# Max pass on 51 contraction rows, two heads at once on the two row halves of TensorE, in a one-core attention layer

## The reference, cut to what matters

```python
xn  = layer_norm(x, norm_w, norm_b)
q   = (xn @ q_w + q_b).reshape(8, 512, 16, 16)
k   = (xn @ k_w + k_b).reshape(8, 512, 16, 16)
att = jnp.einsum('bnhl,bmhl->bnmh', q, k) + (1.0 - mask) * -1000000.0
att = jax.nn.softmax(att, axis=2)
v   = ((xn @ v_w + v_b) * src_mask[:, :, None]).reshape(8, 512, 16, 16)
y   = jnp.einsum('bnmh,bmhl->bnhl', att, v).reshape(8, 512, 256)
h   = layer_norm(y, sb_norm_w, sb_norm_b) * (1.0 + scale) + shift     # scale, shift from silu(cond) @ emb_w
out = x + silu(h) @ out_w + out_b
```

## Time and profile before

| | |
|---|---|
| median of 3 runs | 567.2 us (567.03 to 567.59) |
| profiled execution, its own time | 564.98 us |
| its span | 563.1 us |
| TensorE busy | 96% |
| VectorE busy | 77% |
| ScalarE busy | 66% |
| GpSimd busy | 34% |
| granted TensorE clock | 1.00 throughout |

### The profile page before, as it was taken

One profiled execution on the slowest core, in us unless ns is written; L12 is line 12 of the kernel. 1 busy time (PEld: TensorE's weight loads), 2 busy tenths in 40 slices (PEclk: granted clock), 3 DMA queues, 4 the chain that ended last, 5 costly groups with the idle time before them and its releaser, 6 DMA issues.

```text
span 563.1 us, 10292 instructions
## 1 busy us (share of the span) xinstructions
PE 542.6 (96%) x2845; PEld 226.2 (40%) x2845; DVE 431.7 (77%) x906; ACT 371.2 (66%) x674; POOL 192.7 (34%) x238
## 2 busy tenths in 40 slices
PE   7798999999999999999999999999999999998986
PEld 3452343334443444434443444434443344423334
DVE  7399767987879877897869878897869878788422
ACT  2306866678656886677756786687756786676741
POOL 6433211445225421346205522336215432314003
PEclk9999999999999999999999999999999999999999
DMA  5650342424124333342225243242334223241021
GB/s 140 201 162 11 87 114 86 124 85 123 57 64 139 87 115 103 95 132 79 73 86 141 85 113 104 71 137 79 80 97 132 84 85 90 67 143 34 1 76 37
DMA packets 43433, 53.74 MB, mean 95 GB/s; under 512 B 11000, under 2 KB 36728, under 8 KB 43408
## 3 DMA queue, kind: packets, MB, share of 16 engines
q1 hardware_dynamic: 41360, 53.17, 32.9%
q10 hardware_dynamic: 2048, 0.27, 0.3%
HBM read 36.35 MB, written 16.80 MB: 94 GB/s over the span
## 4 chain that ended last, share of the span: by engine, by line
PE 64%; issue 12%; DMA 7%; DVE 5%; SPq 4%; POOL 3%; ACT 2%; ACTq 1%; POOLq 0%; DVEq 0%
PE pv_ps L414 16%; PE mx_ps L381 15%; PE st_ps L398 14%; PE job_ps L436 6%; DMA q_rows<-qk_dram 5%; PE job_ps L470 4%; PE job_ps L443 3%; SPq L977 2%; DVE negmax L659 2%; POOL qk_parts L855 2%; SPq L980 1%; PE job_ps L458 1%; ACT probs L515 1%; PE job_ps L449 1%; PE job_ps L453 1%
## 5 line engine op out<-in xcount | busy, mean ns | idle before, releaser
L659 DVE TENSOR_REDUCE negmax<-mx_ps 128x1 f32<-128x512 f32 x512 | 328.3, 679 | 74.5 <-PE mx_ps L381 71.3
L515 ACT ACTIVATE probs<-st_ps 128x512 f32<-128x512 f32 x512 | 278.3, 598 | 97.2 <-PE st_ps L398 96.5
L381 PE MATMUL mx_ps<-k_rows,q_rows 99*128 99x512 bf16 x512 | 195.6, 382 | 6.3 <-DMA q_rows<-qk_dram 5.6
L398 PE MATMUL st_ps<-q_rows,k_rows 101*128 101x512 bf16 x512 | 193.7, 381 | 3.3 <-DMA q_rows<-max_parts 1.2
L414 PE MATMUL pv_ps<-probs,v_rows 128*32 128x512 f32 x1024 | 136.4, 605 | 0.5 <-ACT probs L515 0.5
L381 PEld LDWEIGHTS mx_ps<-k_rows,q_rows 99*128 99x128 bf16 x512 | 50.3, 98 | 126.7 <-DVE negmax L659 85.8
L846 POOL TENSOR_TENSOR qk_rest<-qk_full,qk_parts 128x512 f32<-128x512 f32 x32 | 37.0, 1157 | 162.7 <-ACT qk_parts L525 162.6
L398 PEld LDWEIGHTS st_ps<-q_rows,k_rows 101*128 101x128 bf16 x512 | 49.8, 98 | 63.0 <-ACT probs L515 23.5
L855 POOL TENSOR_TENSOR qk_parts<-qk_rest,qk_parts 128x512 bf16<-128x512 f32 x32 | 37.1, 1158 | 68.7 <-DVE qk_parts L736 68.7
L436 PE MATMUL job_ps<-x_norm_t,w_qk 128*128 128x512 f32 x128 | 60.2, 591 | 0.0
L536 ACT ACTIVATE qk_full<-job_ps,qkb_col 128x512 f32<-128x512 f32 x32 | 22.0, 687 | 36.2 <-PE job_ps L436 36.2
(11 more groups left out here) (75 smaller groups left out, 387.8 us busy)
## 6 DMA issues: line engine op xcount, KB each, us to landing
qk_dram<-qk_parts SPq DMA_DIRECT2D x96, 128.0 KB
k_rows<-qk_dram SPq DMA_DIRECT2D x32, 192.0 KB
q_rows<-qk_dram SPq DMA_DIRECT2D x32, 192.0 KB
x_in<-in_x SPq DMA_DIRECT2D x16, 256.0 KB, 3.4
k_rows<-qk_dram SPq DMA_DIRECT2D x32, 128.0 KB
q_rows<-qk_dram SPq DMA_DIRECT2D x32, 128.0 KB
x_res<-in_x SPq DMA_DIRECT2D x8, 512.0 KB, 4.6
out<-out_sb SPq DMA_DIRECT2D x16, 256.0 KB, 2.2
```

What stands on the lines that cost most here:

```text
L381: pe.matmul(mx_ps[bank_of(u, MX_BANKS)][:, :], q_rows[0:ROWS_MASK, g, h, c * P:(c + 1) * P], k_rows[0:ROWS_MASK, g, h, :], start=True, sto ...
L398: pe.matmul(st_ps[bank_of(u, ST_BANKS)][:, :], k_rows[0:ROWS_ALL, g, h, c * P:(c + 1) * P], q_rows[0:ROWS_ALL, g, h, :], start=True, stop= ...
L515: act.activation(probs[:, t % P_SLOTS, h, :], st_ps[bank_of(u, ST_BANKS)][:, :], ACT.Exp).then_inc(exp_done, 1)
L659: dve.tensor_reduce(negmax[:, g % 2, h * CH + c:h * CH + c + 1], mx_ps[bank_of(GH * step + h, MX_BANKS)][:, :], AXIS_X, ALU.max, negate=Tr ...
```

## The change

The max pass now uses three of the six products (part 0 by part 0, part 0 by part 1, part 1 by part 0) and the mask: 48 + 3 = 51 rows, which fit one half (64 rows) of the array. Heads 0 and 1 of a group have their main rows from partition 0, heads 2 and 3 from partition 64. `max_pair` issues the max matmuls of two heads, one on each half, one behind the other (`tile_position=(base, 0)`), into two banks; it waits until both banks are free. The score pass still contracts all six products: for heads 0 and 1 over partitions 0 to 100, for heads 2 and 3 over 0 to 116, of which 0 to 15 are zeros. The heads go in the order 0, 2, 1, 3. A step on TensorE is now: pair, score, score, `pv_step`, MID jobs, pair, score, score, END jobs.

Since the two halves of the heads have different layouts, each fill DMA is now one per half, with 2 KB a row: 12 fills and 2 mask DMAs a group where 6 and 1 were (768 KB in all as before, 32 to 96 KB each), and 4 DMAs on ScalarE for the maxima where 2 were. The large presets of ones are gone; two small tiles are set on VectorE, and ScalarE issues six DMAs that copy them, ahead of its first activation.

```diff
+HALF = 64
+MAIN = 3 * HD
+MASK_AT = MAIN
+MAX_AT = MASK_AT + PARTS
+MAIN_ALL = MAX_AT + 2
+MAIN_BASE = (0, HALF)
+REST_BASE = (MAIN_ALL, HALF - MAIN)
+ROWS_ALL = (MAIN_ALL + MAIN, HALF + MAIN_ALL)
+ORDER = (0, 2, 1, 3)
-ROW_DMAS = 7
+ROW_DMAS = 14
+MAX_DMAS = 4
+PRESET_DMAS = 6
...
-            def max_unit(b, t, h):
+            def max_pair(b, t, j):
...
-                u = GH * step + h
-                wait(pe, max_done, UNITS * mb + bank_before(u, MX_BANKS) + 1)
-                pe.matmul(mx_ps[bank_of(u, MX_BANKS)][:, :], q_rows[0:ROWS_MASK, g, h, c * P:(c + 1) * P],
-                          k_rows[0:ROWS_MASK, g, h, :], start=True, stop=True).then_inc(max_ready, 1)
+                u = GH * step + j
+                freed = max(bank_before(u, MX_BANKS), bank_before(u + 1, MX_BANKS))
+                wait(pe, max_done, UNITS * mb + freed + 1)
+                for half in range(2):
+                    h, base = ORDER[j + half], MAIN_BASE[half]
+                    pe.matmul(mx_ps[bank_of(u + half, MX_BANKS)][:, :],
+                              q_rows[base:base + MAX_AT, g, h, c * P:(c + 1) * P],
+                              k_rows[base:base + MAX_AT, g, h, :], start=True, stop=True,
+                              tile_position=(base, 0)).then_inc(max_ready, 1)
...
+            act.wait_ge(ones_ready, 2)
+            for side, at, count in ((q_rows, MASK_AT, PARTS), (k_rows, MAX_AT, 2)):
+                for half in range(2):
+                    act.dma_start(side[MAIN_BASE[half] + at:MAIN_BASE[half] + at + count, :, 2 * half:2 * half + 2, :]
+                                  .rearrange("p g h t -> p g (h t)"),
+                                  ones_in[0:count, :].unsqueeze(1).broadcast_to((count, NG, 2 * T))).then_inc(rows_preset, 16)
+            for side in (q_rows, k_rows):
+                act.dma_start(side[0:HD, :, 2:4, :].rearrange("p g h t -> p g (h t)"),
+                              zeros_in[:, :].unsqueeze(1).broadcast_to((HD, NG, 2 * T))).then_inc(rows_preset, 16)
...
                     for part in range(2):
-                        act.dma_start(
-                            q_rows[ROWS_MASK + part:ROWS_MASK + part + 1, g, :, :].rearrange(
-                                "p h (c t) -> p (h c) t", t=P),
-                            max_parts[:, i % 2, part:part + 1, :]).then_inc(max_filled[g], 16)
+                        for half in range(2):
+                            row = MAIN_BASE[half] + MAX_AT + part
+                            act.dma_start(
+                                q_rows[row:row + 1, g, 2 * half:2 * half + 2, :].rearrange(
+                                    "p h (c t) -> p (h c) t", t=P),
+                                max_parts[2 * CH * half:2 * CH * (half + 1), i % 2, part:part + 1, :]
+                            ).then_inc(max_filled[g], 16)
...
-                fill(0)
-                fill(1)
-                fill(2)
+                sp.wait_ge(parts_saved[0], 16 * (n + 1))
+                for half in range(2):
+                    main = MAIN_BASE[half]
+                    fill(q_rows, half, main, 2 * HD, of(0, half)[:, 0:1].broadcast_to((HD, 2, 2 * T)))
+                    fill(k_rows, half, main + 2 * HD, HD, of(1, half)[:, 0])
+                sp.wait_ge(parts_saved[1], 16 * (n + 1))
+                for half in range(2):
+                    main = MAIN_BASE[half]
+                    fill(k_rows, half, main, 2 * HD, of(1, half)[:, 0:2])
+                    fill(q_rows, half, main + 2 * HD, HD, of(0, half)[:, 1])
+                sp.wait_ge(parts_saved[2], 16 * (n + 1))
+                for half in range(2):
+                    rest = REST_BASE[half]
+                    fill(k_rows, half, rest, MAIN, of(1, half)[:, 0:PARTS])
+                    fill(q_rows, half, rest, MAIN, of(0, half)[:, ::-1])
```

More of the change, by code:

```diff
@@ L387, in st_unit @@
                 g, c = t // CH, t % CH
-                if c == 0 and h == 0:
-                    pe.wait_ge(max_filled[g], 2 * 16 * (b + 1))
+                if c == 0 and j == 0:
+                    pe.wait_ge(max_filled[g], MAX_DMAS * 16 * (b + 1))
                     if isinstance(b, int) and b == 0 and g == 0:
@@ L394, in st_unit @@
                         pe.wait_ge(cond_ready, 1)
-                u = GH * t + h
+                u, h = GH * t + j, ORDER[j]
+                rows = ROWS_ALL[h // 2]
                 wait(pe, exp_done, UNITS * b + bank_before(u, ST_BANKS) + 1)
-                pe.matmul(st_ps[bank_of(u, ST_BANKS)][:, :], k_rows[0:ROWS_ALL, g, h, c * P:(c + 1) * P],
-                          q_rows[0:ROWS_ALL, g, h, :], start=True, stop=True).then_inc(st_ready, 1)
+                pe.matmul(st_ps[bank_of(u, ST_BANKS)][:, :], k_rows[0:rows, g, h, c * P:(c + 1) * P],
+                          q_rows[0:rows, g, h, :], start=True, stop=True).then_inc(st_ready, 1)
             def pv_step(b, t):
@@ L475, in body @@
                 for t in range(STEPS):
-                    for h in range(GH):
-                        if h == GH // 2:
+                    for j in range(GH):
+                        if j == GH // 2:
                             pv_step(b, t)
@@ L653, in max_unit @@
                     return
-                g, c = step // CH, step % CH
-                if c == 0 and h == 0:
+                g, c, h = step // CH, step % CH, ORDER[j]
+                if c == 0 and j == 0:
                     wait(dve, turned["cturn"], NG * mb + g - 1)
-                dve.wait_ge(max_ready, UNITS * mb + GH * step + h + 1)
-                dve.tensor_reduce(negmax[:, g % 2, h * CH + c:h * CH + c + 1], mx_ps[bank_of(GH * step + h, MX_BANKS)][:, :],
+                dve.wait_ge(max_ready, UNITS * mb + GH * step + j + 1)
+                dve.tensor_reduce(negmax[:, g % 2, h * CH + c:h * CH + c + 1], mx_ps[bank_of(GH * step + j, MX_BANKS)][:, :],
                                   AXIS_X, ALU.max, negate=True).then_inc(max_done, 1)
@@ L693, in split_max @@
                     lap, slot = (b, i - 2) if i >= 2 else (b - 1, i - 2 + NG)
-                    dve.wait_ge(max_filled[slot], 2 * 16 * (lap + 1))
+                    dve.wait_ge(max_filled[slot], MAX_DMAS * 16 * (lap + 1))
                 dve.tensor_copy(max_parts[:, i % 2, 0, :], ps[0:GH * CH, 0:P]).then_inc(split_chain, 1)
@@ L971, in save @@
                                  ).then_inc(parts_saved[part], 16)
-                def fill(part):
-                    sp.wait_ge(parts_saved[part], 16 * (n + 1))
-                    first, count = (0, 3, 5)[part], PARTS - part
-                    sp.dma_start(k_rows[first * HD:(first + count) * HD, i, :, :].rearrange("p h t -> p (h t)"),
-                                 k_src[part].unsqueeze(1).broadcast_to((HD, count, GH * T))).then_inc(rows_filled[i], 16)
-                    first, count = (5, 3, 0)[part], part + 1
-                    sp.dma_start(q_rows[first * HD:(first + count) * HD, i, :, :].rearrange("p h t -> p (h t)"),
-                                 q_src[0:count].rearrange("s l x -> l s x")).then_inc(rows_filled[i], 16)
@@ L985, in spread, with fill @@
-                save(0, part0_ready)
-                sp.dma_start(k_rows[ROWS_PROD:ROWS_MASK, i, :, :],
-                             mask_dram[bass.ds(d, 1)].rearrange("a s t -> (a s) t").unsqueeze(1).broadcast_to(
-                                 (PARTS, GH, T))).then_inc(rows_filled[i], 16)
+                def fill(side, half, first, count, source):
+                    sp.dma_start(side[first:first + count, i, 2 * half:2 * half + 2, :].rearrange("p h t -> p (h t)"),
+                                 source).then_inc(rows_filled[i], 16)
@@ new lines, in of @@
+                def of(side_at, half):
+                    at = side_at * GH + 2 * half
+                    return qk_dram[i, :, :, at:at + 2, :].rearrange("s l h t -> l s (h t)")
+                save(0, part0_ready)
+                for half in range(2):
+                    row = MAIN_BASE[half] + MASK_AT
+                    sp.dma_start(k_rows[row:row + PARTS, i, 2 * half:2 * half + 2, :],
+                                 mask_dram[bass.ds(d, 1)].rearrange("a s t -> (a s) t").unsqueeze(1).broadcast_to(
+                                     (PARTS, 2, T))).then_inc(rows_filled[i], 16)
```

35 lines of the change are left out of this document (16 added, 19 removed).

## The result

The changed kernel takes 647.08 us, median of 4 runs (643.77 to 651.41); the kernel before takes 567.36 us on the same chip (567.03 to 567.59). The ratio is 1.143, 95% interval 1.139 to 1.148. The forecast was 638, the range 604 to 675. The profiled execution is the slowest of the four: 651.41 us, with a span of 649.7.

The account below looks back on a forecast made before the run. The kernel was taken as bound by TensorE and, twice a batch, equally by the row fill. Fill waits of 62 + 3.2 us and 5.8 in the opening, 71 in all, made 636 us profiled, 638 median; range 604 to 675.

Parts of the forecast that it names:

- The fill train: SP's row fills per group: twelve issues 0.63 us apart, 6.93 us instead of 3.15; cast to use 12.3 against 9.04.
- the excess: TensorE's added wait for fills before each group's first max matmul: together 8.85 us a batch.
- The landing: Last fill issue to first max matmul: 2.9 us for 96 KB, between 2.2 (4 KB) and 3.43 (192 KB).
- The total: Whole kernel: 71 us on the profiled execution's 565.0 makes 636; the median of the runs 638.
- The groups' waits: TensorE's fill waits after the opening: 62 us in seven batches, 3.15 us in the last group 3.
- The clock: Rival: TensorE's clock falls in long fill waits, 2 us after each of 15 stalls, 30 us, time 668; chance 0.10.
- clock kept: Forecast case for TensorE: clock stays at full level in the waits, train of 12, halves together; 638 us, chance 0.70.
- The opening: Opening lap: 3.4 us more for group 0, 2.4 for group 1, room in group 2; 5.8 us in all.
- TensorE's gain: Max matmuls as 32 pairs a batch: 7.0 us less 4.8 for tiling, net 2.2, 18 us in 8 batches; hidden by fills.
- a change of tiling: TensorE switching to or from row halves: 0.09 us each, 53 times a batch, 4.8 us; bounds nothing and twice that.
- ScalarE's issues: Two added maxima DMAs a group, 1.2 us, hidden in fill waits: 0; up to 1.2 us for two groups a batch uncovered.
- the signs that the prediction named for being wrong: Fill issues clearly under 0.6 us, last landing far from 2.9, matmuls 0.43 us apart behind a wait, growing max-matmul waits for reduces.

Follow-up runs that it names:

- two-queue kernel: The changed kernel with the second half's six fills issued by GpSimd and the other six by SP: 615.95 us, ratio 1.085.
- the other way of presetting: The changed kernel with ScalarE's six preset DMAs replaced by six memsets, four on GpSimd and two on VectorE: 656.16 us, ratio 1.156.
- two-queue kernels with the opening's fills on SyncE: Changed kernel, fills on two queues, first batch's all on SyncE, GpSimd's x_res add behind h_t: 596.15 us with four maxima DMAs, 585.56 with two.

## Why the prediction was right, point by point

**The fill train, right.** The pitch was given as 0.63 us and is 0.617; the train 6.93 us and is 6.80; the last landing 2.9 and is 2.72; cast to use 12.3 and is 12.0. By group the excess was given as 3.15, 1.25, 1.7 and 2.75 us for groups 3, 0, 1 and 2, and is 2.89, 0.86, 1.96 and 2.70, means of seven; over all 29 groups 65.2 forecast, 62.4 measured. The kernel with nothing but twelve fills shows it is the cause, not only the place. The waits at the max matmuls (26 of them ended by a fill, up to 3.4 us) are those that were named.

**The landing.** 2.72 us for 96 KB lies between the two rows that bounded it, 2.2 us for 4 KB and 3.43 us for 192 KB; taking a value near the middle came out right, without a reason for it. The prediction's 2.2 us for 96 KB, worked out from the Trainium skill, DMA: Bandwidth & Descriptors, Anatomy of one DMA, would have been too low. That page gives its sum for DMAs issued from GpSimd, which the prediction leaves out; for those too the runs disagree, 2.9 to 3.2 us for 96 KB in the two-queue kernel.

**The total, nearer than its terms.** The forecast for the profiled execution was 636 us, and it took 651.4. The groups' waits were put 2.8 us too high, while 18.4 us were not in the sum: 9.8 of clock, 3.3 in the opening and 5.3 in the end. Against the median the forecast is only 9 us short because the profiled execution is the slowest of the four, 4.3 us above that median.

**The clock, a rival that came in part.** It was given 0.10 and 30 us. It fell in some of the waits and not in others, and cost 9.8 us between first pairs and casts, some 0.7 at the end, and in the opening an amount that no run separates (17 us at 0.50). The step that was mis-sized is the forecast's "clock kept", zero, and the rival's two bounds (0 and 60 us) hold it. The Trainium skill, TensorE: Matmul & The Clock Gate, HAM oscillation, tells of a kernel whose clock fell in every one of its waits for a DMA; here nine of 29 groups show it (first pair to next cast 8.43 instead of 6.90 us at the longest). Matmuls on the warm-up tile (0, 5, 11 and 7 of them) took it away: in that kernel the clock stood at 1.00 from 90 to 580 us.

**The opening, too small.** 5.8 us forecast, 9.1 measured. Two terms were put at nothing. One is the six preset DMAs on ScalarE, beside the loads at no cost: with them ScalarE's table load comes 6.6 us later, SP's last loads 2 us and the first save 2.2 us. The other is the clock, which stood at 0.50 for 17 us of the opening. How the missing 3.3 us divide between the two stays open, since the other way of presetting brought a delay of its own and the clock differed between the executions.

**TensorE's gain: hidden, as forecast; without the fills there is none.** The prediction put it at 18 us if TensorE alone set the time, with 0.09 us for a change of tiling. The change costs that: pair to score matmul is 0.32 us instead of 0.22, and the two matmuls start together, so the arithmetic on TensorE was right. Halves against the full array give 7 to 9 us, about the half of 18 that the prediction allowed where VectorE's reduces hold the pairs back. What wasn't counted is the joint wait for two banks, which costs some 10 us. With the fills as before the whole gain is 0 (567.01 us). Of the signs that the prediction named for being wrong one came, small: the waits of max matmuls' weight loads for reduces grew, from 85.8 us in all to 94.1.

**ScalarE's issues, right with its condition.** Nothing while the fill wait covers them, up to 1.2 us for two groups a batch if the cover were gone, which makes 17 us in seven batches; measured 10.6 us by the medians, 14 by the ratios. Missed was the end, where no fill wait follows: the last group's two added issues are exposed and make some 2 of the last 5.3 us.

## What to carry to other kernels

Count DMA issues on the chain, not bytes: cutting a transfer in two doubles its share of a train, and here that alone cost 13%, some clock included. Before a layout buys time on one engine, ask what each buffer it fills is made of and who issues that. And when a wait is shortened, look at what had been hidden in it: two added DMAs went from costing nothing to 10 us or more, and an add on another engine came beside an instruction that it trebled.

## What the runs showed that I had not expected

- GpSimd issues a fill in 0.51 to 0.54 us (medians), a little less than SP's 0.55 to 0.59, but 96 KB land 2.9 to 3.2 us behind it; on SP it is 2.72 us from the last issue to the matmul that waits for it.
- h_t on VectorE (two SBUF inputs, 128x512) takes 0.68 us alone, 1.4 to 1.5 beside a GpSimd instruction of 1.16 us, and 3.25 beside one of 2.37.
- Three of SP's issues of loads, at 7.17, 8.15 and 9.71 us, took 0.93, 1.52 and 1.07 us in the changed kernel, against 0.61, 0.61 and 0.47 in the kernel before. ScalarE had issued its last preset DMA by 7.4 us, but the transfers of its queue took 54% of the DMA engines' time from 7 to 11 us.
- In the opening the clock differs between executions of nearly the same program: of the two-queue kernels with the opening's fills on SyncE the one with four maxima DMAs stood at 0.50 there for 7 us, the one with two for 34. A few us in one execution's opening are therefore no measure of a change.
